# Exponentials taken two PSUM banks at a time in an attention loop

## What is computed

```python
attn = jnp.einsum('bhqd,bhkd->bhqk', query, key) / scale
attn = jax.nn.softmax(attn, axis=-1)
out = jnp.einsum('bhqk,bhkd->bhqd', attn, value)
...
out = out.transpose(0, 2, 1, 3).reshape(b, s, d_model)
return out @ Wo_w + Wo_b
```

## Time and profile before

| what | us |
| --- | --- |
| median of three runs | 440.38 |
| lowest and highest run | 436.19, 443.81 |
| the profiled execution, its own time | 442.51 |
| span of the profiled execution, first to last instruction | 440.7 |
| attention steps 0 to 13 in it | 79.7 to 227.4 |

### The profile page before, as it was taken

How to read it: one execution, slowest core, us unless ns; L and a number is a source line. 1 busy time by engine, 2 the same in 40 slices (tenths; PEclk the granted TensorE clock), 3 DMA queues, 4 the chain that set the end, 5 groups by cost and what they waited for, 6 DMA issues and landing times.

```text
span 440.7 us, 7483 instructions
## 1 busy us (share of the span) xinstructions
PE 325.5 (74%) x2383; PEld 153.8 (35%) x2383; DVE 283.5 (64%) x569; ACT 200.4 (45%) x377; POOL 163.1 (37%) x188
## 2 busy tenths in 40 slices
PE   5699537899999999999999895310357898870940
PEld 3353103333333333333334354300224575540630
DVE  4987997798999999999967614678642324220210
ACT  2413330588888888888877520100032223220110
POOL 2607751151111111111113602100084788888672
PEclk9999957899999999999999959555586999896785
DMA  7302675011111111111005000001422565454232
GB/s 235 79 0 71 204 238 175 32 39 38 39 38 38 38 44 40 39 43 47 10 1 146 26 0 25 1 0 59 138 63 61 136 137 135 90 94 82 27 30 18
DMA packets 34344, 30.39 MB, mean 69 GB/s; under 512 B 5264, under 2 KB 28560, under 8 KB 34320
## 3 DMA queue, kind: packets, MB, share of 16 engines
q1 hardware_dynamic: 28176, 23.65, 17.3%
q0 software_dynamic: 6144, 6.43, 9.3%
HBM read 18.27 MB, written 11.60 MB: 68 GB/s over the span
## 4 chain that ended last, share of the span: by engine, by line
PE 45%; DVE 16%; POOL 15%; issue 12%; ACT 4%; DMA 3%; another core or an unknown queue 1%; SPq 0%; DVEq 0%; ACTq 0%; POOLq 0%
PE ps L1160 14%; PE ps L1123 8%; POOL out L494 8%; PE ps L1146 6%; DVE mx L787 5%; POOL ex L483 4%; PE ps L1349 3%; DVE big L901 3%; PE ps L1381 2%; PE ps L1173 2%; ACT osb L576 2%; PE ps L1247 2%; PE ps L1213 1%; DMA ex<-rows,idx 1%
## 5 line engine op out<-in xcount | busy, mean ns | idle before, releaser
L787 DVE TENSOR_REDUCE mx<-ps 128x2 f32<-128x1024 f32 x128 | 148.3, 1217 | 9.7 <-PE ps L1123 9.4
L599 ACT ACTIVATE big<-ps 128x512 f32<-128x512 f32 x256 | 139.4, 597 | 32.3 <-PE ps L1146 30.2
L1160 PE MATMUL ps<-big,VA 128*32 128x256 f32 (+1 forms) x960 | 82.0, 413 | 2.3 <-ACT osb L576 2.3
L1123 PE MATMUL ps<-KB,QB 48*128 48x512 bf16 x256 | 52.0, 405 | 12.5 <-DVE mx L787 9.8
L1146 PE MATMUL ps<-QB,KB 51*128 51x512 bf16 x256 | 55.9, 386 | 2.9 <-ACT big L599 1.3
L494 POOL DMA_INDIRECT out<-big,idx x32 | 50.6, 1582 | 14.0 <-issue 8.8
L483 POOL DMA_INDIRECT ex<-rows,idx x32 | 34.4, 1073 | 57.4 <-DVE idx L1010 43.2
L645 ACT ACTIVATE big<-ps,b1c 128x512 f32<-128x512 f32 x32 | 22.0, 687 | 63.4 <-PE ps L1349 59.0
L1349 PE MATMUL ps<-big,w1s 128*128 128x512 f32 x64 | 36.3, 687 | 2.8 <-DVE big L973 1.7
L413 POOL COPY VA<-Vall 128x128 f32 (+1 forms) x16 | 4.6, 290 | 82.8 <-PE ps L1160 82.8
L1123 PEld LDWEIGHTS ps<-KB,QB 48*128 48x128 bf16 x256 | 12.3, 93 | 58.1 <-DVE mx L787 30.8
(11 more groups left out here) (164 smaller groups left out, 419.9 us busy)
## 6 DMA issues: line engine op xcount, KB each, us to landing
KB<-k_parts SPq DMA_DIRECT2D x32, 96.0 KB
QB<-q_parts SPq DMA_DIRECT2D x32, 96.0 KB
w1s<-in_w SPq DMA_DIRECT2D x8, 256.0 KB
w2s<-in_w SPq DMA_DIRECT2D x8, 256.0 KB
k_parts<-big SPq DMA_DIRECT2D x4, 384.0 KB, 3.2
q_parts<-big SPq DMA_DIRECT2D x4, 384.0 KB, 4.1
QB<-mxp SPq DMA_DIRECT2D x96, 2.0 KB
rows<-rw SPq DMA_DIRECT2D x1, 1088.0 KB, 6.0
```

The costliest lines, as they stand in the source:

```text
L599: nc.scalar.activation(PT[:, u, 2 * i + half, kc, :], ps[:, banks[n], :], ACT.Exp, scale=SCALE).then_inc(s_ex, 1)
L787: nc.vector.tensor_reduce(mx[:, u, :].rearrange("p (h a) -> p h a", h=2)[:, :, n], ps[:, max_bank(u, n):max_bank(u, n) + 2, :], AX.X, ALU.max,
L1123: ins = mm(ps[:, max_bank(u, n) + half, :], QB[rows, r, i, qc * 128:(qc + 1) * 128], KB[rows, r, i, :], start=True, stop=True)
L1160: ins = mm(ps[32 * j:32 * j + 32, 6, cols], VA[:, u, kc, j, :], PT[:, u, j, kc, cols], start=kc == 0 and not cols.start, stop=kc == TC - 1 ...
```

## The change

The sixteen exponentials of a step are no longer sixteen instructions of 512 elements. `EXP_GROUPS` lists ten: blocks (0,1), 2, (3,4), (5,6), 7, (8,9), 10, (11,12), 13, (14,15). A pair is one instruction of 1024 elements over banks 4 and 5, a single is one of 512 over bank 7. The exponential waits until all blocks of its group are there, and counts `s_ex` up by its width when it is done.

On PE the first block of a group waits for the last group of the same width (the one that used the same banks); the second block of a pair has no wait. Block 2 waits for the last single of the step before, block 7 for the copy of the maxima. `max_turn` is moved from ahead of unit 1 to ahead of unit 2 and also waits for exponential 2 of the step; `max_out` is moved from ahead of block 2 to ahead of group (5,6), that is behind pair (3,4). The buffer `PT` is laid out by block number n, so that a pair is one run of 1024 elements, and `weigh` reads it in that order. Steps 14 and 15 use `EXP_SINGLE`, which is what they did before.

```diff
-EXP_BANKS = [(4, 5)[n] if n < 2 else (4, 5, 7)[(n + 1) % 3] for n in range(2 * 2 * TC)]
+EXP_GROUPS = ((0, 2), (2, 1), (3, 2), (5, 2), (7, 1), (8, 2), (10, 1), (11, 2), (13, 1), (14, 2))
+EXP_SINGLE = tuple((n, 1) for n in range(2 * 2 * TC))
+MAX_OUT_AT = 5
...
-        PT = big[:, :].rearrange("p (u j c q) -> p u j c q", u=2, j=4, c=TC)
+        PT = big[:, :].rearrange("p (u n q) -> p u n q", u=2, n=4 * TC)
...
-                for n in range(16):
+                for n, width in groups:
...
-                    if n == 2 and more_max:
+                    if n == MAX_OUT_AT and more_max:
                         max_out(s + 1)
...
-                    act.wait_ge(s_sc, 16 * s + n + 1)
-                    nc.scalar.activation(PT[:, u, 2 * i + half, kc, :], ps[:, banks[n], :], ACT.Exp,
-                                         scale=SCALE).then_inc(s_ex, 1)
+                    act.wait_ge(s_sc, 16 * s + n + width)
+                    bank = 4 + n % 2 if groups is EXP_SINGLE else 4 if width == 2 else 7
+                    nc.scalar.activation(PT[:, u, n:n + width, :], ps[:, bank:bank + width, :], ACT.Exp,
+                                         scale=SCALE).then_inc(s_ex, width)
...
+                if not (isinstance(s, int) and (s < 2 or s == NS - 1)):
+                    pe.wait_ge(s_ex, 16 * (s - 1) + 3)
                 nc.tensor.transpose(ps[0:16, 7, 0:128], mx[:, u, :], ident[:]).then_inc(s_mt, 1)
...
-                if banks is EXP_BANKS and n == 4:
-                    pe.wait_ge(s_mn, s + 2)
-                elif banks is EXP_BANKS and n > 4:
-                    pe.wait_ge(s_ex, 16 * s + n - 2)
-                elif not (isinstance(s, int) and 16 * s + n < 2):
+                first = isinstance(s, int) and s == 0
+                if groups is EXP_SINGLE:
+                    bank = 4 + n % 2
                     pe.wait_ge(s_ex, 16 * s + n - 1)
+                else:
+                    at = next(g for g, (m, w) in enumerate(groups) if m <= n < m + w)
+                    m, width = groups[at]
+                    bank = 7 if width == 1 else 4 + n - m
+                    if n == 7 and first:
+                        pe.wait_ge(s_ex, 3)
+                    elif n == 7:
+                        pe.wait_ge(s_mn, s + 2)
+                    elif n == m and at >= 2:
+                        k = max(g for g in range(at) if groups[g][1] == width)
+                        pe.wait_ge(s_ex, 16 * s + sum(groups[k]))
+                    elif n == 0 and not first:
+                        pe.wait_ge(s_ex, 16 * s)
...
+                    elif n == 2:
+                        pe.wait_ge(s_ex, 16 * s - 2)
...
-                    if n == 1 and turn:
+                    if n == 2 and turn:
                         max_turn(s + 1, 1 - u)
```

More of the change, by code:

```diff
@@ L582, in gates_out, with step @@
                 nc.scalar.activation(ge[:, cols], ps[:, 1, cols], ACT.Exp, scale=-1.0).then_inc(s_ge, 1)
-            def step(s, u, prev=True, more_max=True, last=False, banks=EXP_BANKS):
-                for n in range(16):
+            def step(s, u, prev=True, more_max=True, last=False, groups=EXP_GROUPS):
+                for n, width in groups:
                     if n == 0 and prev:
                         out_copy(s - 2)
-                    if n == 2 and more_max:
+                    if n == MAX_OUT_AT and more_max:
                         max_out(s + 1)
@@ L594, in step @@
                         gates_out(n // 8)
-                    i, kc, half = n // 8, (n // 2) % 4, n % 2
                     if n == 0 and not (isinstance(s, int) and s < 2):
                         act.wait_ge(s_pv, s - 1)
-                    act.wait_ge(s_sc, 16 * s + n + 1)
-                    nc.scalar.activation(PT[:, u, 2 * i + half, kc, :], ps[:, banks[n], :], ACT.Exp,
-                                         scale=SCALE).then_inc(s_ex, 1)
+                    act.wait_ge(s_sc, 16 * s + n + width)
+                    bank = 4 + n % 2 if groups is EXP_SINGLE else 4 if width == 2 else 7
+                    nc.scalar.activation(PT[:, u, n:n + width, :], ps[:, bank:bank + width, :], ACT.Exp,
+                                         scale=SCALE).then_inc(s_ex, width)
             max_out(0)
@@ L608, in _ @@
                 step(it * 2 + 1, 1)
-            step(14, 0, banks=(4, 5) * 8)
-            step(15, 1, more_max=False, last=True, banks=(4, 5) * 8)
+            step(14, 0, groups=EXP_SINGLE)
+            step(15, 1, more_max=False, last=True, groups=EXP_SINGLE)
             out_copy(15)
@@ L1130, in max_turn, with exp_unit @@
                     pe.wait_ge(s_mn, s)
+                if not (isinstance(s, int) and (s < 2 or s == NS - 1)):
+                    pe.wait_ge(s_ex, 16 * (s - 1) + 3)
                 nc.tensor.transpose(ps[0:16, 7, 0:128], mx[:, u, :], ident[:]).then_inc(s_mt, 1)
-            def exp_unit(q, r, n, banks=EXP_BANKS):
+            def exp_unit(q, r, n, groups=EXP_GROUPS):
                 s = q * 4 + r
@@ L1138, in exp_unit @@
                     pe.wait_ge(l_e[r], (q + 1) * 96)
-                if banks is EXP_BANKS and n == 4:
-                    pe.wait_ge(s_mn, s + 2)
-                elif banks is EXP_BANKS and n > 4:
-                    pe.wait_ge(s_ex, 16 * s + n - 2)
-                elif not (isinstance(s, int) and 16 * s + n < 2):
-                    pe.wait_ge(s_ex, 16 * s + n - 1)
+                first = isinstance(s, int) and s == 0
+                if groups is EXP_SINGLE:
+                    bank = 4 + n % 2
+                    pe.wait_ge(s_ex, 16 * s + n - 1)
+                else:
[11 more added lines that the diff above has]
+                        pe.wait_ge(s_ex, 16 * s)
+                    elif n == 2 and first:
+                        pe.wait_ge(s_mn, 2)
+                    elif n == 2:
+                        pe.wait_ge(s_ex, 16 * s - 2)
                 rows = slice(64 * half, 64 * half + PR + 3)
-                mm(ps[:, banks[n], :], KB[rows, r, i, kc * 128:(kc + 1) * 128], QB[rows, r, i, :],
+                mm(ps[:, bank, :], KB[rows, r, i, kc * 128:(kc + 1) * 128], QB[rows, r, i, :],
                    start=True, stop=True).then_inc(s_sc, 1)
@@ L1159, in weigh @@
                 for j in range(4):
-                    ins = mm(ps[32 * j:32 * j + 32, 6, cols], VA[:, u, kc, j, :], PT[:, u, j, kc, cols],
+                    ins = mm(ps[32 * j:32 * j + 32, 6, cols], VA[:, u, kc, j, :], PT[:, u, 2 * TC * (j // 2) + 2 * kc + j % 2, cols],
                              start=kc == 0 and not cols.start, stop=kc == TC - 1 and cols.stop == L)
@@ L1247, in stay_warm, with step @@
                     mm(ps[:, 6, 0:256], warm_x[:, 0:128], warm_x, start=True, stop=True)
-            def step(q, r, prev=True, prev2=True, more_max=True, turn=True, beside=None, banks=EXP_BANKS):
+            def step(q, r, prev=True, prev2=True, more_max=True, turn=True, beside=None, groups=EXP_GROUPS):
                 s, u = q * 4 + r, r % 2
                 for n in range(8):
-                    if n == 1 and turn:
+                    if n == 2 and turn:
                         max_turn(s + 1, 1 - u)
@@ L1258, in step @@
                         max_unit(q + (r + 2) // 4, (r + 2) % 4, n)
-                    exp_unit(q, r, 2 * n, banks)
-                    exp_unit(q, r, 2 * n + 1, banks)
+                    exp_unit(q, r, 2 * n, groups)
+                    exp_unit(q, r, 2 * n + 1, groups)
                     if prev:
@@ L1288, in _ @@
             pe.wait_ge(s_prep, 4)
-            step(3, 2, more_max=False, beside=beside_14, banks=(4, 5) * 8)
+            step(3, 2, more_max=False, beside=beside_14, groups=EXP_SINGLE)
             for n in range(8):
@@ L1293, in _ @@
                     out_turn(13, LAST_TURN)
-                exp_unit(3, 3, 2 * n, (4, 5) * 8)
-                exp_unit(3, 3, 2 * n + 1, (4, 5) * 8)
+                exp_unit(3, 3, 2 * n, EXP_SINGLE)
+                exp_unit(3, 3, 2 * n + 1, EXP_SINGLE)
                 if n < TC:
```

## The result

The changed kernel takes 491.74 us (median of 4 runs, 486.26 to 494.80) against 440.82 before. The ratio is 1.113, 95% interval 1.106 to 1.119. It is slower, as forecast, but by 50.9 us and not by 34, and outside the stated range of 464 to 487.

A forecast was written before the change was run, and what follows sets the result against it. DVE was taken to set the pace (10.17 us of a 10.50 us step), PE following with 0.76 in hand. Steps of 13.01 us and the first and last steps' additions summed to 34.2 us: 474.5 us, range 464 to 487.

The forecast's parts named there:

- The walk round a step: Attention loop on PE, score matmul to score matmul: waits and work sum to 13.01 us a step, against 10.50.
- The five round trips: PE's waits for pair exponentials before blocks 3, 5, 11, 14 and the next 0: 1.51 to 1.55 us each.
- the extra wait of the turn: Between blocks 3 and 4, the maxima's turn also waits for exponential 2, ending 0.1 us late: 1.42 instead of 1.32.
- Step 1: Second step of the loop, without output turn and copy: about 12.75 us, +2.6.
- A rule that speaks against the sum: PE clock in the loop: the skill's rule says partly 1.2 GHz; the prediction held that by the trace it is not.
- rival 1: The clock falls in the loop: 21.0 us steps at 1.2 GHz, half of 14 steps, about 530 us; chance 0.05.
- the two bounds of the range: Pair exponential's length in the loop: at 0.93 us the kernel takes 467 us, at 1.20 us 486.
- The prediction's own sign of being wrong: Wrong if block 5 follows 4 at once, the loop's clock is below 1.00, or block 0 waits for a DMA.
- the 0.76 us: PE's claimed room in each loop step before the change: 9.74 us of own work in a 10.50 us step.
- Rival 2: PE's room swallows all waits but block 4 to 5: 0.75 us a step, 10.5 in all, 451 us; chance 0.05.
- rival 3: Not slower: block 5's wait is over when PE arrives, DVE keeps the pace at 10.17 us, 436 us; chance 0.03.
- The maxima's path: Copy behind pair (3,4), GpSimd, small DMAs to the next block 0: 11.5 us, hidden by 1.5 in a 13.0 step.

The follow-up runs named there:

- e3: Changed kernel with unit 3's maxima matmuls issued four extra times between blocks 4 and 5, changing no result; 475.39 us, ratio 1.088 to the kernel before.
- e5: Kernel before (single banks) with block 5 waiting for exponential 4 in place of 2; 451.91 us, ratio 1.034.
- e8: Kernel before with two score matmuls (0.43 us) added at the step's head, between block 1 and the first weigh, into bank 7; 437.00 us, ratio 1.004.
- e1: Kernel before with only the PT layout changed to block number; 438.97 us against 438.58, ratio 1.001.
- e2: Changed kernel with each pair's exponential cut in two 512-element instructions, semaphore counted behind the second; ratio 1.102 to the kernel before.
- e6: Kernel before with the turn of the maxima behind block 3 and its copy ahead of exponential 3; 436.78 us against 437.70, ratio 0.998.

## Why the prediction was wrong, point by point

**The walk round a step** held. Forecast 13.01 us, measured 13.15 where nothing disturbs a step. The terms are in the trace, start to start: block 0 to 3 1.60 (forecast 1.53), 3 to 4 1.32 (1.42, the extra wait of the turn did not arise), 4 to 5 1.55 (1.51), 5 to 6 1.12 (1.11), 6 to 8 1.72 (1.76), 8 to 11 1.59 (1.51), 11 to 12 1.11, 12 to 14 1.55 (1.51), 14 to the next 0 1.60 (1.55). The five round trips together take 0.28 us more than forecast, about half of it from the pair's later start (0.05 each, less 0.02 for the shorter pair); the turn's wait that did not arise and the output turn give 0.13 back, so in part the sum came out by errors of both signs. Step 1 was further off, 13.54 in place of 12.75, also with the clock held (13.53 in e3). With the clock at 1.00 (e3) the loss is 475.39 - 438.58 = 36.8 us, against a forecast of 34.2; that would have been inside the range.

**The step that failed** is in "A rule that speaks against the sum": "sparser work than the changed loop, and the clock held ... by the trace it is not". The stretch from 228 to 241 was no witness: its row gives PE as busy for 12.87 of 13.00 us, while an undisturbed step of the changed kernel has 11.14 of 13.20. I had called it sparser because matmuls were missing in it, and did not read the busy column next to the clock that I quoted. Two rows of the same trace spoke the other way. The row next to it covers more of the single-bank steps, and its clock is 0.78; and the half clock at 79.71 stands right behind a bare wait of 1.32 us, which the prediction mentions for rival 1 and gave no weight:

```profile
241.00:264.00 23.00, 21.72 (x129) 10.29 (x132) 8.63 (x25) 9.34 (x19) 7.97 (x8) 0.78 0.09 28
```
```profile
79.03 0.35 PE L1131 MATMUL ps<-ident,mx 128*16 128x128 f32 x1 [1.32 <-DVE mx L787]
79.31 0.61 PE L1123 MATMUL ps<-KB,QB 48*128 48x512 bf16 x2
```

The changed loop leaves TensorE bare for 1.18 us in one piece in every step, and behind it the clock fell in seven steps of one profile, at 1.2 to 2.5 us each. Filled, it did not fall at all. Of the 48.8 us that the loop lost (196.5 - 147.7), 36.9 are the waits (184.6 in e3) and 11.9 the clock; by the medians the clock's part is 14. It is what takes the time out of the range: the two bounds of the range came from the length of the pair alone, and the clock stood in the sum at nothing. The prediction's own sign of being wrong, a granted clock below 1.00 in the loop, came true. The Trainium skill (TensorE: Matmul & The Clock Gate, "A second HAM failure mode: psum-queue depth-cycling"), whose rule I set aside with a chance of 0.05, describes this case: short idles between groups of matmuls while PSUM banks are cycled. Here the trace agrees with it, with a clock of 0.57 from 136 to 144. My rival had the right mechanism and too large a price (530 us, half of the steps wholly at the lower level). Half of the steps were touched, which was a guess that happened to fit, and each only in part.

**What bounds the kernel before** was misread too, without harm to the sum. "DVE sets the pace now, PE follows with 0.76 us in hand": e5 to e8 show that the 0.76 us cannot be spent. The walk did not use them, since it followed the waits themselves. Rival 2, which did use them, fell with e5, and rival 3 with the rows of the changed kernel: block 5 comes 1.55 us or more after block 4 in every step of the loop.

**Other edits.** The layout is free (e1). The maxima's path stayed hidden: its copy ends at 152.25, 4.6 us into the step as forecast, and no step of the profile of the changed kernel begins with a wait for a DMA. ACT's saving is worth nothing, as forecast, and as a round trip the pair is not even shorter than two singles (e2).

## What to carry to other kernels

Fusing instructions over more banks hands the banks over later and all at once; before it, walk once round the loop and count who can write what meanwhile, above all where two groups of the same banks stand next to each other. Idle time on an engine is room only if work put there is hidden, so add a little work at two places and compare: here the same 0.43 us cost 5.5 us in one place and almost nothing in the other. And a wait that leaves TensorE bare has a second price, the clock: read the busy column beside the granted clock, and if the wait can't go, put work into it.

## What the runs showed that I had not expected

- A two-bank exponential starts 0.47 us after its matmul, a single 0.42, and takes 1.02 us against 1.08 for two singles in a row (0.49 apart); the round trip is 1.55 us either way.
- Added matmuls with no use made a kernel 12 us faster by its loop and 14 by the medians (e3 against the changed kernel).
- The clock fell to half in seven of fourteen steps, each time within 1.6 us of the end of a 1.18 us bare wait. With the bare wait at 0.69 us (e5) it fell in none of the steps after the first. Why it fell in some steps with the same wait and not in others stays open; the wait of 1.32 us at the loop's start is also followed by a fall in the profile of the kernel before and by none in those of e6 and e8.
